# The exponential's shift in an attention kernel, made by one VectorE pass over the scores in place of a maximum and an addition

## The chip, the cores and the metric

One core of one Trainium2 chip runs the whole program. The metric is the device time of one execution in microseconds, as the median of the runs of a kernel. The engines are named as in the profile: PE is TensorE's matmuls, PEld its weight loads, DVE is VectorE, ACT is ScalarE, POOL is GpSimd, SP is the queue that issues most of the DMAs.

## What is computed

For each of 32 batches, 112 latents (`x`, normalized) attend to 375 context rows and to themselves (487 keys), with 16 heads of 64 dimensions; then comes a routed feed-forward layer of 8 experts. The part that matters here is the softmax:

```
q = lat @ Wq;  k, v = split(concatenate([ctx, lat]) @ Wkv)
dots = einsum('bhid,bhjd->bhij', q, k) * scale          # 112 x 487 per head
attn = softmax(dots, axis=-1)
out  = einsum('bhij,bhjd->bhid', attn, v) @ Wout
x    = x + tanh(g_xattn) * out
```

The exponential is taken of a score less its row's maximum, plus a constant, `P_SHIFT` = 14 ln 2, which drops out when a row is divided by its sum.

## The kernel before

The program is `attention()`, which ends at about 1363 us, and then `routed_ffn()`, which the change does not touch. Attention works in steps `t`; a step is one pair of heads (two heads, h = 0 and 1) of a batch, so a batch has 8 steps, j = 0 to 7. All engines walk the same list of steps (L639 for PE, L502 for DVE, L376 for ACT, L288 for POOL, L208 for SP), each with its own program written out by hand in a fixed order; semaphores tie them together. Nothing is reordered at run time.

Precision is made of pieces: q and k are split into a high part, which ACT copies out of PSUM, and a low part, which DVE computes as PSUM less the high part (`k_lo` L530, `q_lo` L518). V is split likewise (`v_sb` L416 on ACT, L536 on DVE), and so is P (`p_parts`: L374 on ACT, L279 on POOL).

In an even step t PE makes the scores of two pairs, t and t+1, into four PSUM banks (L653), after `exp_done` says that the banks are free. Then, in every step, PE projects K and V for the same pair of the next batch (L635, twelve matmuls in all), and multiplies P of pair t - 4 by V (L684, L686). In steps with j = 2 and 4 it transposes the normalized inputs of the batch after the next (L719, L720, called T), and in steps with j = 3 and 7 it projects half of Q. K, V, T and Q units share two PSUM banks, `proj_ps`, in turn: the function `take` (L617) makes a unit wait until the unit before the last has been read out by its last reader. So the K projection of an odd step waits for `k_lo` of the even step before it; T waits for `k_lo` of its own step, and the K projection after T waits for the low part of V.

DVE's order in an even step is: `q_lo` if due (j = 0 and 4), four maxima (L495, one per bank) with two additions of `P_SHIFT` among them (L500, each over two columns of `neg_max`), then `k_lo`, then the low part of V, then the rest. L500 waits for the semaphore `max_done` of DVE's own maxima. ACT's order in an even step is: high part of K, exponential h = 0, high part of V, attention output's high part (L424), exponential h = 1. In the odd step: exponential h = 0, K, exponential h = 1, V, and then the four copies of P (L374), of which two fall in the next even step. An exponential writes `p_f` in SBUF and its row sum through the accumulator, which the trace shows as a second instruction (ACTIVATION_READ_ACCUMULATOR, L365). ACT waits for `bias_done` ahead of h = 0 alone.

SP transposes P of two pairs in each even step by DMA (L217), once POOL has made their low parts.

Of the kernel before, what the change touches and what calls it, by code (L numbers as in the profile page):

```python
# [6 lines left out]
F16 = mybir.dt.float16  # L7
I32 = mybir.dt.int32
U32 = mybir.dt.uint32
ALU = mybir.AluOpType  # L10
ACT = mybir.ActivationFunctionType
AX = mybir.AxisListType

NB, LQ, LC, D = 32, 112, 375, 256
H, DH = 16, 64
LK = LC + LQ
# [11 lines left out]
P_SHIFT = 14 * 0.6931471805599453  # L28
# [5 lines left out]
def span(t):  # L34

    return t // NP, t % NP
# [6 lines left out]
def is_pair(p):  # L43
    return 0 <= p < PAIRS


def is_batch(b):
    return 0 <= b < NB
# [20 lines left out]
def attention(nc, x, ctx_in, g_x, ln_m_g, ln_m_b, ln_l_g, ln_l_b, wq, wkv, wout, gate_w, x2_out, xn_out, top_v, top_i, ident, w1, w2, peaks):  # L69
    with ExitStack() as st:  # L70
        sb = lambda name, shape, dt=F32: st.enter_context(nc.sbuf_tensor(name, shape, dt))
        sem = lambda name: st.enter_context(nc.semaphore(name))
# [18 lines left out]
        scale = scale_i[:, 0].bitcast(F32)  # L91
        inverse = scale_i[:, 1].bitcast(F32)
        undo = sb("att_undo", [128, 6])
# [17 lines left out]
        p_f = sb("p_f", [128, 2, 2, 512])  # L111
        p_parts = sb("p_parts", [128, PS, 2, 2, 512], F16)
        pt_sb = sb("pt_sb", [128, PS, 16 * LQ + 16], F16)
        neg_max = sb("neg_max", [128, 2, 4])
        shift = sb("shift", [128, 2, 4])
        row_sum = sb("row_sum", [128, 4, 4])
        inv_sum = sb("inv_sum", [128, 4, 4])
# [16 lines left out]
        scores_ps = [bank(f"scores_ps{n}") for n in range(4)]  # L134
# [12 lines left out]
        proj_done = sem("proj_done")  # L147
        kq_high = sem("kq_high"); kq_low = sem("kq_low"); v_high = sem("v_high"); v_low = sem("v_low")
        kv_affine = sem("kv_affine"); kvhi_done = sem("kvhi_done"); kvlo_done = sem("kvlo_done")
        scores_done = sem("scores_done"); max_done = sem("max_done"); bias_done = sem("bias_done"); exp_done = sem("exp_done")  # L150
        p_high = sem("p_high"); p_low = sem("p_low"); p_moved = [sem(f"p_moved{n}") for n in range(PS)]
        pv_done = sem("pv_done"); inv_done = sem("inv_done"); o_summed = sem("o_summed"); o_scaled = sem("o_scaled"); o_high = sem("o_high"); o_low = sem("o_low")
        o_moved = [sem("o_moved0"), sem("o_moved1")]
# [11 lines left out]
        def unit_ready(kind, index):  # L165

            n = UNIT_NUMBER[kind, index]
            return n + 1, proj_ps[n % 2]
# [181 lines left out]
        @block.scalar  # L350
        def _(act):
            act.wait_ge(small_loaded, 16 * 6)
            act.activation(tanh_g[:, :], tanh_g[:, :], ACT.Tanh).then_inc(tanh_done, 1)
            act.wait_ge(scales_ready, 1)
            for k in range(KD):
                act.activation(wkv_hi[:, k], stage[:, k], ACT.Copy, scale=scale[:, 0:1]).then_inc(w_high, 1)

            def exponential(p, h):
                if h == 0:
                    act.wait_ge(bias_done, p + 1)  # L360
                    if p >= 2:

                        act.wait_ge(p_low, 2 * (p - 2) + 2)
                n = 2 * (p % 2) + h
                act.activation(p_f[0:LQ, p % 2, h, 0:LK], scores_ps[n][0:LQ, 0:LK], ACT.Exp, bias=shift[0:LQ, p // 2 % 2, n:n + 1],  # L365
                               accum_out=row_sum[0:LQ, p // 2 % 4, n:n + 1]).then_inc(exp_done, 1)

            def p_high_of(p):
                if p >= PS:

                    act.wait_ge(p_moved[p % PS], 16 * (p // PS))
                for h in range(2):
                    act.wait_ge(exp_done, 2 * p + h + 1)
                    act.activation(p_parts[0:LQ, p % PS, h, 0, 0:LK], p_f[0:LQ, p % 2, h, 0:LK], ACT.Copy).then_inc(p_high, 1)  # L374

            for t in STEPS:  # L376
                b, j = span(t)
                qb = b if j == 0 else b + 1
                if t == -NP - 2:
                    act.activation(wq_hi[:, :, :], stage_q, ACT.Copy, scale=scale[:, 1:2]).then_inc(w_high, 1)  # L380
                    act.activation(wout_hi[:, :, :], stage_out, ACT.Copy, scale=scale[:, 2:3]).then_inc(w_high, 1)
                if t == 0:
                    act.wait_ge(set_up, 2)
                if j in (0, 4) and is_batch(qb):

                    n = 1 if j == 0 else 0
                    done, ps = unit_ready("Q", 2 * qb + n)
                    act.wait_ge(proj_done, done)
                    act.activation(q_hi[:, 4 * n:4 * n + 4], ps[:, 0:4 * LQ].rearrange("p (m q) -> p m q", m=4), ACT.Copy,
                                   scale=undo[:, 0:1]).then_inc(kq_high, 1)  # L390
                if t % 2 == 0 and is_pair(t - 1):
                    p_high_of(t - 1)
                ob = out_batch(t, 3 * NP + 2)
                if ob is not None:
                    act.wait_ge(xnt_done, ob + 1)
                    act.activation(xnt_sb[:, :, :], tail_ps[:, 0:KD * LQ].rearrange("p (k q) -> p k q", k=KD), ACT.Copy).then_inc(xnt_copied, 1)
                if t % 2 == 1 and is_pair(t):
                    exponential(t, 0)
                if is_pair(t + NP):
                    done, ps = unit_ready("K", t + NP)  # L400
                    act.wait_ge(proj_done, done)
                    act.activation(k_hi[:, j], ps[:, 0:LKP], ACT.Copy).then_inc(kq_high, 1)  # L402
                if j in (3, 5) and is_batch(b + 2):
                    k = (j - 3) // 2
                    act.wait_ge(kv_affine, 2 * (b + 2) + k + 1)
                    act.activation(kv_hi[:, b % 2, k], kv_f[:, k], ACT.Copy).then_inc(kvhi_done, 1)
                if is_pair(t):
                    exponential(t, t % 2)
                if is_pair(t + NP):
                    done, ps = unit_ready("V", t + NP)  # L410
                    act.wait_ge(proj_done, done)
                    c, half_ = j % KT, j // KT
                    rows = 128 if c < KT - 1 else LKP - 128 * (KT - 1)
                    if b in (-1, 0) and j == 0:
                        act.wait_ge(v_cleared, b + 2)
                    act.activation(v_sb[0:rows, (b + 1) % 2, c, 8 * half_:8 * half_ + 8, 0], ps[0:rows, :].rearrange("p (n d) -> p n d", d=DH),  # L416
                                   ACT.Copy, scale=V_SCALE).then_inc(v_high, 1)
                g = (t - LAG - 2) // 2
                if t % 2 == 0 and 0 <= g < PAIRS // 2:
                    ob, n = g // 4, g % 4  # L420
                    act.wait_ge(o_scaled, g + 1)
                    if n == 0 and ob >= 2:
                        act.wait_ge(o_moved[ob % 2], 16 * (ob // 2))
                    act.activation(o_parts[0:LQ, ob % 2, 0, 4 * DH * n:4 * DH * (n + 1)], o_f[0:LQ, g % 2].rearrange("p h d -> p (h d)"), ACT.Copy).then_inc(o_high, 1)  # L424
                if t % 2 == 0 and is_pair(t):
                    exponential(t, 1)
                if t % 2 == 1 and is_pair(t - 1):
                    p_high_of(t - 1)

        @block.vector  # L430
        def _(dve):
# [4 lines left out]
            def then(instruction):  # L436
                n_step[0] += 1
                instruction.then_inc(scale_step, 1)

                dve.wait_ge(scale_step, n_step[0])  # L440

            def weight_scales():
# [27 lines left out]
                then(dve.tensor_scalar(affine[:, :, :].rearrange("p a k -> p (a k)"), affine[:, :, :].rearrange("p a k -> p (a k)"), scale[:, 3:4], None, ALU.mult))  # L470
                then(dve.tensor_tensor(undo[:, 2:3], inverse[:, 3:4], inverse[:, 0:1], ALU.mult))
                then(dve.tensor_scalar(undo[:, 3:4], undo[:, 2:3], inverse[:, 2:3], 1.0 / V_SCALE, ALU.mult, ALU.mult))
                then(dve.tensor_scalar(undo[:, 4:5], undo[:, 2:3], inverse[:, 3:4], float(DH) ** -0.5, ALU.mult, ALU.mult))
                then(dve.tensor_scalar(undo[:, 0:1], undo[:, 4:5], inverse[:, 1:2], None, ALU.mult))
                dve.wait_ge(tanh_done, 1)
                then(dve.tensor_scalar(undo[:, 1:2], undo[:, 3:4], tanh_g[:, :], None, ALU.mult))
# [12 lines left out]
                dve.wait_ge(w_high, 4)  # L489
                dve.scalar_tensor_tensor(out=wout_lo[:, :, :], in0=stage_out, scalar=scale[:, 2:3], in1=wout_hi[:, :, :], op0=ALU.mult, op1=ALU.subtract).then_inc(w_ready, 1)  # L490

            def maximum(p, h):
                n = 2 * (p % 2) + h
                dve.wait_ge(scores_done, 2 * p + h + 1)
                dve.tensor_reduce(neg_max[0:LQ, p // 2 % 2, n:n + 1], scores_ps[n][0:LQ, 0:LK], AX.X, ALU.max, negate=True).then_inc(max_done, 1)  # L495

            def bias(p):
                n = 2 * (p % 2)
                dve.wait_ge(max_done, 2 * p + 2)
                dve.tensor_scalar(shift[0:LQ, p // 2 % 2, n:n + 2], neg_max[0:LQ, p // 2 % 2, n:n + 2], P_SHIFT, None, ALU.add).then_inc(bias_done, 1)  # L500

            for t in STEPS:  # L502
                b, j = span(t)
                nb = b + 2
                if t == -3 * NP + 2:
                    weight_scales()
# [7 lines left out]
                if j in (0, 4) and is_batch(qb):  # L514
                    n = 1 if j == 0 else 0
# [2 lines left out]
                    dve.scalar_tensor_tensor(out=q_lo[:, 4 * n:4 * n + 4], in0=ps[:, 0:4 * LQ].rearrange("p (m q) -> p m q", m=4), scalar=undo[:, 0:1],  # L518
                                             in1=q_hi[:, 4 * n:4 * n + 4].bitcast(F32), op0=ALU.mult, op1=ALU.subtract).then_inc(kq_low, 1)
                if t % 2 == 0 and is_pair(t):  # L520
                    maximum(t, 0)
                    maximum(t, 1)
                    maximum(t + 1, 0)
                    bias(t)
                    maximum(t + 1, 1)
                    bias(t + 1)
                if is_pair(t + NP):
                    done, ps = unit_ready("K", t + NP)
                    dve.wait_ge(kq_high, kq_count("K", t + NP))
# [789 lines left out]
```

## Time and profile before

| | us |
|---|---|
| median of 3 runs | 1902.32 |
| lowest and highest | 1900.02, 1903.77 |
| the profiled execution, its own time | 1902.62 |
| its span | 1900.9 |
| PE busy in the span | 1674.2 (88%) |
| DVE busy | 1428.0 (75%) |
| ACT busy | 1195.3 (63%) |
| POOL busy | 1183.0 (62%) |

The span in 40 equal slices shows attention up to slice 28 or so and the feed-forward layer behind it:

```profile
PE   2899999999999999999999999998402999999980
DVE  4777888888888888888888888877395666666646
ACT  2587777777777777877777777777254333433320
POOL 4477777777777777777777777767263343333320
PEclk9999999999999999999999999999555999999995
```

Each digit is the busy share of a slice in tenths, and the last line is the clock granted to TensorE. Times of a trace are counted from the span's start. A matmul's recorded length is modelled and longer than the distance to the next one, so a gap on PE is best read from starts, or from the idle time ahead of a weight load.

### The profile page before, as it was taken

The page shows a single profiled execution, that of the slowest core. Times are in us where ns is not written, and L with a number is a line of the kernel's source. Part 1 is how long each engine was busy: PE and PEld are TensorE (multiplying, and loading weights), DVE is VectorE, ACT ScalarE, POOL GpSimd, SP SyncE. Part 2 cuts the span into 40 slices and gives each one's busy share as a digit, 9 for nine tenths or more (in the row PEclk, how much of TensorE's full clock was granted, in tenths as well). Part 3 has the DMA queues.
Part 4 walks back from the last instruction along what each step waited for, and adds up shares of the span by engine and source line. Part 5 has one row for each costly group of instructions (what it writes and reads, how often), then busy time and mean ns, then how long its engine had stood idle before and what let it go on. Part 6 is the DMA issues. An engine that isn't in the chain of part 4 may idle for free. (4 is left out here: it accounts for less than half of the span.)

```text
span 1900.9 us, 42714 instructions
## 1 busy us (share of the span) xinstructions
PE 1674.2 (88%) x15031; PEld 1163.1 (61%) x15032; DVE 1428.0 (75%) x2917; ACT 1195.3 (63%) x2666; POOL 1183.0 (62%) x1297
## 2 busy tenths in 40 slices
PE   2899999999999999999999999998402999999980
PEld 1456666666666666666666666665302999989970
DVE  4777888888888888888888888877395666666646
ACT  2587777777777777877777777777254333433320
POOL 4477777777777777777777777767263343333320
PEclk9999999999999999999999999999555999999995
DMA  3267766767767666676776776767455111111119
GB/s 131 46 127 140 142 144 131 139 139 142 147 129 145 138 140 144 135 139 138 139 150 136 136 137 129 138 130 142 118 186 173 46 49 45 50 50 47 47 35 289
DMA packets 599541, 233.18 MB, mean 123 GB/s; under 512 B 534064, under 2 KB 584016, under 8 KB 598992
## 3 DMA queue, kind: packets, MB, share of 16 engines
q1 hardware_dynamic: 592656, 212.67, 52.5%
q0 software_dynamic: 6720, 18.36, 3.1%
q8 instruction: 98, 1.61, 0.3%
q14 instruction: 67, 0.55, 0.1%
HBM read 78.66 MB, written 20.19 MB: 52 GB/s over the span
## 5 line engine op out<-in xcount | busy, mean ns | idle before, releaser
L279 POOL TENSOR_TENSOR p_parts<-p_f,p_parts 112x487 f16<-112x487 f32 x512 | 560.4, 1118 | 194.2 <-ACT p_parts L374 194.2
L365 ACT ACTIVATE p_f<-scores_ps,shift 112x487 f32<-112x487 f32 x512 | 337.0, 663 | 13.3 <-DVE shift L500 9.7
L495 DVE TENSOR_REDUCE neg_max<-scores_ps 112x1 f32<-112x487 f32 x512 | 313.0, 654 | 27.1 <-PE scores_ps L653 27.1
L402 ACT ACTIVATE k_hi<-proj_ps 128x488 fp32r<-128x488 f32 x256 | 147.9, 578 | 262.5 <-PE proj_ps L635 262.5
L1018 ACT ACTIVATE space<-h_ps,b_sb,undo 128x256 f32<-128x256 f32 x280 | 142.8, 560 | 232.1 <-PE h_ps L1247 228.8
L374 ACT ACTIVATE p_parts<-p_f 112x487 f16<-112x487 f32 x512 | 275.9, 607 | 0.0
L536 DVE SCALAR_TENSOR_TENSOR v_sb<-proj_ps,v_sb 128x512 f16<-128x512 f32 (+1 forms) x256 | 176.5, 689 | 92.1 <-ACT v_sb L416 89.4
L530 DVE TENSOR_TENSOR k_lo<-proj_ps,k_hi 128x488 fp32r<-128x488 f32 x256 | 168.2, 657 | 78.2 <-ACT k_hi L402 78.0
L684 PE MATMUL pv_ps<-v_sb,pt_sb 128*128 128x128 f16 x2048 | 218.9, 221 | 7.8 <-DMA pt_sb<-p_parts 7.8
L635 PE MATMUL proj_ps<-kv_hi,wkv_hi 128*128 128x488 f16 x512 | 192.3, 376 | 22.0 <-POOL kv_lo L306 13.5
L635 PE MATMUL proj_ps<-wkv_hi,kv_hi 128*128 128x512 f16 (+1 forms) x512 | 194.6, 380 | 0.1
L635 PE MATMUL proj_ps<-wkv_lo,kv_hi 128*128 128x512 f16 (+1 forms) x512 | 194.6, 380 | 0.0
L635 PE MATMUL proj_ps<-wkv_hi,kv_lo 128*128 128x512 f16 (+1 forms) x512 | 194.6, 380 | 0.0
L635 PE MATMUL proj_ps<-kv_lo,wkv_hi 128*128 128x488 f16 x512 | 189.7, 370 | 0.0
L635 PE MATMUL proj_ps<-kv_hi,wkv_lo 128*128 128x488 f16 x512 | 189.5, 370 | 0.0
L1270 PE MATMUL y_ps<-w_hi,stage 128*128 x1120 | 189.0, 273 | 0.0
L989 POOL DMA_INDIRECT y_rows<-space,y_row_i x70 | 69.6, 994 | 152.0 <-DVE space L1187 141.3
L416 ACT ACTIVATE v_sb<-proj_ps 128x512 f16<-128x512 f32 (+1 forms) x256 | 152.5, 596 | 16.9 <-PE proj_ps L635 6.4
L1247 PE MATMUL h_ps<-xt_hi,w_hi 128*128 128x256 f16 x560 | 154.4, 276 | 4.3 <-DVE xt_lo L1179 4.3
L684 PEld LDWEIGHTS pv_ps<-v_sb,pt_sb 128*128 128x128 f16 x2048 | 135.1, 99 | 37.6 <-DMA pt_sb<-p_parts 8.9
L1247 PE MATMUL h_ps<-xt_lo,w_hi 128*128 128x256 f16 x560 | 154.5, 276 | 0.0
L1247 PE MATMUL h_ps<-xt_hi,w_lo 128*128 128x256 f16 x560 | 154.3, 276 | 0.0
(222 smaller groups left out, 4075.1 us busy)
## 6 DMA issues: line engine op xcount, KB each, us to landing
w_part<-in_L_ffn_w_dram SPq DMA_DIRECT2D x64, 256.0 KB, 3.5
stage<-in_L_ffn_w_dram SPq DMA_DIRECT2D x32, 512.0 KB, 4.1
ctx_sb<-in_ctx_dram SPq DMA_DIRECT2D x32, 375.0 KB
space<-y_rows SPq DMA_DIRECT2D x32, 224.0 KB, 4.7
pt_sb<-p_parts SPq DMA_TRANSPOSE x256, 4.0
x_sb<-in_x_dram SPq DMA_DIRECT2D x32, 112.0 KB
res_sb<-in_x_dram SPq DMA_DIRECT2D x32, 112.0 KB, 5.3
x_dram<-x_sb SPq DMA_DIRECT2D x32, 112.0 KB, 2.9
```

Source lines behind the costliest of these rows:

```text
L279: pool.tensor_tensor(p_parts[0:LQ, p % PS, h, 1, 0:LK], p_f[0:LQ, p % 2, h, 0:LK], p_parts[0:LQ, p % PS, h, 0, 0:LK], ALU.subtract).then_i ...
L365: act.activation(p_f[0:LQ, p % 2, h, 0:LK], scores_ps[n][0:LQ, 0:LK], ACT.Exp, bias=shift[0:LQ, p // 2 % 2, n:n + 1], accum_out=row_sum[0: ...
L374: act.activation(p_parts[0:LQ, p % PS, h, 0, 0:LK], p_f[0:LQ, p % 2, h, 0:LK], ACT.Copy).then_inc(p_high, 1)
L402: act.activation(k_hi[:, j], ps[:, 0:LKP], ACT.Copy).then_inc(kq_high, 1)
L416: act.activation(v_sb[0:rows, (b + 1) % 2, c, 8 * half_:8 * half_ + 8, 0], ps[0:rows, :].rearrange("p (n d) -> p n d", d=DH), ACT.Copy, sc ...
L495: dve.tensor_reduce(neg_max[0:LQ, p // 2 % 2, n:n + 1], scores_ps[n][0:LQ, 0:LK], AX.X, ALU.max, negate=True).then_inc(max_done, 1)
L530: dve.tensor_tensor(k_lo[:, j], ps[:, 0:LKP], k_hi[:, j].bitcast(F32), ALU.subtract).then_inc(kq_low, 1)
L536: dve.scalar_tensor_tensor(out=v_of(1), in0=ps[0:rows, :].rearrange("p (n d) -> p n d", d=DH), scalar=V_SCALE, in1=v_of(0), op0=ALU.mult, ...
L635: last = nc.tensor.matmul(out, lhs(a, k), rhs(c, k), start=(n == 0), stop=(n == 3 * KD - 1))
L684: last = nc.tensor.matmul(pv_ps[:, at:at + 128], block_of(0, c), v_sb[:, sv, c, n].rearrange("p a d -> p (a d)"), start=(c == 0), stop=(c ...
L1247: last = nc.tensor.matmul(h_ps[m][:, c * ROWS:c * ROWS + ROWS], (w1_hi, w1_lo)[a][:, k, bass.ds(e1, 1), f:f + 128].rearrange("p o f -> p ( ...
L1270: last = nc.tensor.matmul(y_ps[s][:, r * D:r * D + D], (g_hi, g_lo)[a][:, s, m, c, r * 128:r * 128 + 128], (w2_hi, w2_lo)[b][:, m * 2 + c, ...
```

## The change

The maximum of a row and the addition of `P_SHIFT` become one instruction, a tensor_scalar with an accumulator output: it adds `P_SHIFT` to each score, writes the 112 x 487 result as float16 into a new SBUF tile, `passed`, that nothing reads, and accumulates the minimum of what it passes. So that a minimum serves, the scores are negated: the factor `undo[:, 4]`, from which q's scale is made, gets a minus sign, and the exponential reads its input with scale -1. ACT now waits for `shift_done` ahead of each exponential.

```
-  then(dve.tensor_scalar(undo[:, 4:5], undo[:, 2:3], inverse[:, 3:4], float(DH) ** -0.5, ALU.mult, ALU.mult))
+  then(dve.tensor_scalar(undo[:, 4:5], undo[:, 2:3], inverse[:, 3:4], -float(DH) ** -0.5, ALU.mult, ALU.mult))
...
   def exponential(p, h):
-      if h == 0:
-          act.wait_ge(bias_done, p + 1)
-          if p >= 2:
-              act.wait_ge(p_low, 2 * (p - 2) + 2)
+      act.wait_ge(shift_done, 2 * p + h + 1)
+      if h == 0 and p >= 2:
+          act.wait_ge(p_low, 2 * (p - 2) + 2)
       act.activation(p_f[...], scores_ps[n][0:LQ, 0:LK], ACT.Exp, bias=shift[...],
+                     scale=-1.0,
                      accum_out=row_sum[...]).then_inc(exp_done, 1)
...
-  def maximum(p, h):
+  def shifted_minimum(p, h):
       n = 2 * (p % 2) + h
       dve.wait_ge(scores_done, 2 * p + h + 1)
-      dve.tensor_reduce(neg_max[...], scores_ps[n][0:LQ, 0:LK], AX.X, ALU.max, negate=True).then_inc(max_done, 1)
-  def bias(p):
-      n = 2 * (p % 2)
-      dve.wait_ge(max_done, 2 * p + 2)
-      dve.tensor_scalar(shift[..., n:n + 2], neg_max[..., n:n + 2], P_SHIFT, None, ALU.add).then_inc(bias_done, 1)
+      dve.tensor_scalar(passed[0:LQ, n], scores_ps[n][0:LQ, 0:LK], P_SHIFT, None, ALU.add, ALU.min,
+                        accum_out=shift[..., n:n + 1]).then_inc(shift_done, 1)
...
   if t % 2 == 0 and is_pair(t):
-      maximum(t, 0)
-      maximum(t, 1)
-      maximum(t + 1, 0)
-      bias(t)
-      maximum(t + 1, 1)
-      bias(t + 1)
+      for p in (t, t + 1):
+          for h in range(2):
+              shifted_minimum(p, h)
```

## Rows read from the trace of the kernel before

**Rows 1.** The page's first line.

```profile
span 1900.9 us, 42714 instructions
```

**Rows 2.** Busy time by stretch: us, each engine's busy us, granted clock, DMA share.

```profile
700.00:1000.00 300.00, 296.85 (x2698) 188.32 (x2696) 251.08 (x559) 234.61 (x552) 230.76 (x264) 1.00 0.70 141
```

**Rows 3.** Groups of DVE instructions, 100 to 1300 us: busy us, mean ns, idle before.

```profile
L495 DVE TENSOR_REDUCE neg_max<-scores_ps 112x1 f32<-112x487 f32 x484 | 295.8, 654 | 21.1 <-PE scores_ps L653 21.1
L500 DVE TENSOR_SCALAR shift<-neg_max 112x2 f32<-112x2 f32 x242 | 95.1, 393 | 4.2
```

**Rows 4.** Waits of PE's weight loads, 100 to 1300 us: total, times, longest.

```profile
PEld proj_ps L635 <- DVE k_lo L530: 15.7, 61, 1.7
PEld proj_ps L719 <- DVE k_lo L530: 15.7, 29, 0.6
```

**Rows 5.** Timeline of DVE and PEld in a step with j = 0: start, us.

```profile
709.14 1.80 DVE L495 TENSOR_REDUCE neg_max<-scores_ps 112x1 f32<-112x487 f32 x3
710.86 0.17 DVE L500 TENSOR_SCALAR shift<-neg_max 112x2 f32<-112x2 f32 x1
710.94 0.65 DVE L495 TENSOR_REDUCE neg_max<-scores_ps 112x1 f32<-112x487 f32 x1
711.62 0.47 DVE L500 TENSOR_SCALAR shift<-neg_max 112x2 f32<-112x2 f32 x1
712.01 0.65 DVE L530 TENSOR_TENSOR k_lo<-proj_ps,k_hi 128x488 fp32r<-128x488 f32 x1
...
712.71 0.10 PEld L635 LDWEIGHTS proj_ps<-kv_hi,wkv_hi 128*128 128x128 f16 x1 [0.22 <-DVE k_lo L530]
```

**Rows 6.** Timeline of POOL in the same step.

```profile
709.89 2.19 POOL L279 TENSOR_TENSOR p_parts<-p_f,p_parts 112x487 f16<-112x487 f32 x2
```

**Rows 7.** Timeline of DVE, ACT and PEld in the step with j = 4.

```profile
727.76 1.80 DVE L495 TENSOR_REDUCE neg_max<-scores_ps 112x1 f32<-112x487 f32 x3
...
730.95 0.65 DVE L530 TENSOR_TENSOR k_lo<-proj_ps,k_hi 128x488 fp32r<-128x488 f32 x1
731.53 0.67 DVE L536 SCALAR_TENSOR_TENSOR v_sb<-proj_ps,v_sb 128x512 f16<-128x512 f32 x1
...
730.57 0.19 ACT L365 ACTIVATION_READ_ACCUMULATOR p_f<-scores_ps,shift 112x1 f32 x1
730.66 0.59 ACT L416 ACTIVATE v_sb<-proj_ps 128x512 f16<-128x512 f32 x1
...
731.66 0.31 PEld L719 LDWEIGHTS proj_ps<-ident,norm_sb 125*128 125x128 f32 x3 [0.55 <-DVE k_lo L530]
...
732.25 0.10 PEld L635 LDWEIGHTS proj_ps<-kv_hi,wkv_hi 128*128 128x128 f16 x1 [0.18 <-DVE v_sb L536]
```

**Rows 8.** Timeline of DVE, ACT and PEld in the step with j = 6.

```profile
739.14 1.81 DVE L495 TENSOR_REDUCE neg_max<-scores_ps 112x1 f32<-112x487 f32 x3 [0.72 <-PE scores_ps L653]
...
742.39 0.65 DVE L530 TENSOR_TENSOR k_lo<-proj_ps,k_hi 128x488 fp32r<-128x488 f32 x1
...
741.15 0.58 ACT L402 ACTIVATE k_hi<-proj_ps 128x488 fp32r<-128x488 f32 x1 [3.24 <-PE proj_ps L635]
...
743.10 0.10 PEld L635 LDWEIGHTS proj_ps<-kv_hi,wkv_hi 128*128 128x128 f16 x1 [0.19 <-DVE k_lo L530]
```

**Rows 9.** Timeline of DVE and PE in the step with j = 2.

```profile
717.64 1.77 DVE L495 TENSOR_REDUCE neg_max<-scores_ps 112x1 f32<-112x487 f32 x3
...
720.40 0.65 DVE L530 TENSOR_TENSOR k_lo<-proj_ps,k_hi 128x488 fp32r<-128x488 f32 x1
...
721.34 0.52 PE L719 MATMUL proj_ps<-ident,norm_sb 125*128 125x125 f32 x3
```

**Rows 10.** Groups of DVE instructions in the feed-forward layer, 1450 to 1900 us.

```profile
L1177 DVE TENSOR_SCALAR xt_hi<-xt_ps 128x512 f16<-128x512 f32 x35 | 23.9, 682 | 7.3 <-PE xt_ps L1256 7.3
```

**Rows 11.** The last batch: an ACT wait (1296 to 1363 us) and a stretch.

```profile
ACT p_f L365 <- DVE shift L500: 6.1, 4, 2.2
...
1310.00:1320.00 10.00, 8.36 (x77) 6.71 (x78) 6.00 (x12) 7.36 (x20) 7.40 (x8) 0.69 0.94 202
```

More of the change, by code:

```diff
@@ L113, in attention @@
         pt_sb = sb("pt_sb", [128, PS, 16 * LQ + 16], F16)
-        neg_max = sb("neg_max", [128, 2, 4])
+        passed = sb("passed", [128, 4, LK], F16)
         shift = sb("shift", [128, 2, 4])
@@ L149, in attention @@
         kv_affine = sem("kv_affine"); kvhi_done = sem("kvhi_done"); kvlo_done = sem("kvlo_done")
-        scores_done = sem("scores_done"); max_done = sem("max_done"); bias_done = sem("bias_done"); exp_done = sem("exp_done")
+        scores_done = sem("scores_done"); shift_done = sem("shift_done"); exp_done = sem("exp_done")
         p_high = sem("p_high"); p_low = sem("p_low"); p_moved = [sem(f"p_moved{n}") for n in range(PS)]
@@ L358, in exponential @@
             def exponential(p, h):
-                if h == 0:
-                    act.wait_ge(bias_done, p + 1)
-                    if p >= 2:
-                        act.wait_ge(p_low, 2 * (p - 2) + 2)
+                act.wait_ge(shift_done, 2 * p + h + 1)
+                if h == 0 and p >= 2:
+                    act.wait_ge(p_low, 2 * (p - 2) + 2)
                 n = 2 * (p % 2) + h
-                act.activation(p_f[0:LQ, p % 2, h, 0:LK], scores_ps[n][0:LQ, 0:LK], ACT.Exp, bias=shift[0:LQ, p // 2 % 2, n:n + 1],
+                act.activation(p_f[0:LQ, p % 2, h, 0:LK], scores_ps[n][0:LQ, 0:LK], ACT.Exp, bias=shift[0:LQ, p // 2 % 2, n:n + 1], scale=-1.0,
                                accum_out=row_sum[0:LQ, p // 2 % 4, n:n + 1]).then_inc(exp_done, 1)
@@ L490, in split_out_weights @@
                 dve.scalar_tensor_tensor(out=wout_lo[:, :, :], in0=stage_out, scalar=scale[:, 2:3], in1=wout_hi[:, :, :], op0=ALU.mult, op1=ALU.subtract).then_inc(w_ready, 1)
-            def maximum(p, h):
+            def shifted_minimum(p, h):
                 n = 2 * (p % 2) + h
                 dve.wait_ge(scores_done, 2 * p + h + 1)
-                dve.tensor_reduce(neg_max[0:LQ, p // 2 % 2, n:n + 1], scores_ps[n][0:LQ, 0:LK], AX.X, ALU.max, negate=True).then_inc(max_done, 1)
-            def bias(p):
-                n = 2 * (p % 2)
-                dve.wait_ge(max_done, 2 * p + 2)
-                dve.tensor_scalar(shift[0:LQ, p // 2 % 2, n:n + 2], neg_max[0:LQ, p // 2 % 2, n:n + 2], P_SHIFT, None, ALU.add).then_inc(bias_done, 1)
+                dve.tensor_scalar(passed[0:LQ, n], scores_ps[n][0:LQ, 0:LK], P_SHIFT, None, ALU.add, ALU.min,
+                                  accum_out=shift[0:LQ, p // 2 % 2, n:n + 1]).then_inc(shift_done, 1)
             for t in STEPS:
```

## The prediction

> **What bounds the kernel now.** The page gives a span of 1900.9 us [rows 1]; the execution's own time is 1902.6, within 0.02% of the median of the runs (1902.3), so the sum below is made against 1902.6. The view by stretches shows that attention is TensorE's: in 300 us it is busy for 296.9, at the full granted clock, while DVE is busy for 251 and ACT for 235 [rows 2]. A faster DVE can therefore only give back what PE loses by waiting for DVE. The view of the waits shows two such groups of PE's weight loads, both on `k_lo`: 15.7 us ahead of projections and 15.7 us ahead of transposes [rows 4]. That is the pool from which the change can draw, some 31 us in 1200, and the timelines show why `k_lo` is late: it stands behind the four maxima and the two additions.
>
> **What the block costs now.** From the first maximum to `k_lo` it is 712.01 - 709.14 = 2.87 us at j = 0 [rows 5], 720.40 - 717.64 = 2.76 at j = 2 [rows 9], 3.19 at j = 4 [rows 7] and 3.25 at j = 6 [rows 8]. Three maxima take from 709.14 to 710.86, that is 0.573 from start to start, though one is recorded with 0.654 [rows 3, 5]. Four would be 2.29, so the additions and their waits cost 0.47 to 0.96 a block. That is a lot for two columns each. The mean addition lasts 393 ns [rows 3], and the short one took 0.17, with the next maximum 0.08 after its start; the long one lasted from 711.62 to 712.09 [rows 5], and POOL's two subtractions lasted from 709.89 to 712.08 [rows 6]. The short one ended at 711.03, in the middle of POOL's two, where one gives way to the other. The addition goes from SBUF to SBUF, and it looks as if it stood until POOL's instruction was over.
>
> The Trainium skill, SBUF — State Buffer, has in the section on the shared ports that a tensor_scalar in a two-port mode and a GpSimd instruction block each other fully, whichever came first, and that the form with an accumulator output is not among the ops that do. By that rule the long additions are waits for a port, and the new form, which has one, waits for none; the trace agrees on the first half, and nothing in it shows the second.
>
> **What the change adds.** The pass itself: the nearest row is a tensor_scalar from PSUM to float16, 682 ns for 512 columns [rows 10], against 654 for a maximum over 487 [rows 3]; the 25 columns more account for the 28 ns at about 1 ns each, so I take the same 0.573 from start to start. Beside it comes the reading of the accumulator, which no DVE row shows. Below, it could cost nothing. Above, it could wait for the recorded end of the pass (0.654 - 0.573 = 0.08 later) and then take its own 0.2, as ACT's does by its recorded length: 0.28. On ACT the next instruction starts 0.09 after that reading (730.57 to 730.66) [rows 7], and DVE's short addition let the next one start after 0.08 [rows 5]; I take 0.08, since both rows are of that kind of short instruction. A block is then 4 x (0.573 + 0.08) = 2.61 us.
>
> The Trainium skill, VectorE: DVE Perf Modes, speaks against such fusing: its section on the DRAIN says that the next op starts only when the pipe is empty, and that one should lower the number of ops; its section on two Vector instructions with no wait between them counts an accumulator output as an instruction of its own. A block would go from six instructions to eight. The maxima here start 0.08 ahead of the recorded end of the one before, so the trace does not show a full drain; if the reading had one, the block would be near the upper bound, which is the slower rival below.
>
> **What each step of a batch gives.** At j = 0, `k_lo` starts 0.26 earlier (2.87 - 2.61). The K projection of the next step idles 0.22 for it [rows 5], so all of the 0.22 goes. At j = 6, `k_lo` could start 0.64 earlier, at 741.75; the high part of K is done at 741.73 [rows 8], so that does not hold it up. The 0.19 of idle time goes whole. At j = 4, `k_lo` starts 0.58 earlier, at 730.37, and the 0.55 ahead of the transposes goes [rows 7]. But a part comes back: the K projection after them waits for the low part of V, which now ends at 732.20 and releases PE at 732.25. It follows ACT's high part, over at 731.25, so it can run from about 731.28 to 731.96 and release PE at 732.01: 0.24 is left of the 0.55. That is the new wait, on ACT in place of DVE. If ACT's copy came earlier too, since its exponential no longer waits for an addition, the most would be 0.54, where the 0.59 of transposes [rows 7] starts straight after the products with V. At j = 2, `k_lo` ends at 721.05 and the transposes start at 721.34 anyway [rows 9]: nothing, and 0.2 us of slack. The odd steps have no block. Sum: 0.22 + 0.19 + 0.24 = 0.65 us a batch. K is projected beside the scores in 31 of the 32 batches: 20.2 us.
>
> **What costs nothing.** The negation is a sign in a constant and a scale in an instruction that ACT runs anyway. The wait ahead of the second exponential is met long before, as ACT comes to it over 1 us after the pass. DVE's float16 writes into `passed` have no reader, and no DMA is touched. What covers the first exponential in the body is the K copy ahead of it. In the last batch there is no projection, and ACT does wait for the addition: 6.1 us in four waits [rows 11]. With the change the first exponential needs one pass of 0.65 instead of three and an addition. But the DMA engines that transpose P are 0.94 busy there [rows 11], so most of it will turn into waiting for them. I credit 2 us, between 0 and 6.1.
>
> **The sum:** 1902.6 - 20.2 - 2.0 = 1880.4; against the median 0.3 less, and I say 1880.5.
>
> **Rivals.** (A) *The reading of the accumulator is dear* and DVE becomes later than it was. At 0.28 each a block is 4 x 0.853 = 3.41 us, and `k_lo` comes 0.54, 0.65, 0.22 and 0.16 later at j = 0, 2, 4 and 6. The slack of 0.2 at j = 2 takes its part off: 0.54 + 0.45 + 0.22 + 0.16 = 1.37 a batch, 42 us, so 1945. The point from which it decides: at 0.19 a block is 3.05, which loses 0.18 and 0.09 at j = 0 and 2 and gains some 0.14 and 0.19 at j = 4 and 6, about nothing. For it speaks that no DVE row shows the instruction; against it that the twin on ACT lets the next one start after 0.09. Chance 0.12.
> (B) *A middling price*, about 0.15: the block is 2.89 and j = 0 gives nothing (2.87 before), while j = 4 and 6 give 0.24 and 0.19: 0.43 x 31 = 13.3, and 1 at the end, so 1888. The same time comes out if the price is small and PE meets another wait at one of the steps. Chance 0.20.
> (C) *Nothing reaches PE*, because another reader of the two banks is late wherever `k_lo` was: 1902 within 4 us. Against it: the three waits named are put down to `k_lo` in 90 cases [rows 4]. Chance 0.08. That the additions stay in another form is excluded by the diff, which takes the instructions out.
>
> **Numbers.** The forecast has 0.60. The low end: 0.22 + 0.19 + 0.54 for 31 batches and 6.1 at the end would be 1867; all of these together is unlikely, and I set 1872. The high end takes in (B) with a price up to 0.18: 1898. What is left out is (A) and most of (C). A measurement of this kernel can tell 0.2% (3.8 us) from no change; faster by more: 0.60 + 0.20 = 0.80, the same 0.08, slower 0.12.
>
> **What would show it.** In the profile after: a second DVE instruction behind each pass, with the next pass 0.65 after the one before; `k_lo` 2.6 us after the block's start at all j alike, since POOL no longer sets its length; the waits for `k_lo` ahead of L719 and L635 gone or below 3 us each, and the one for the low part of V still there, but put down to ACT's copy; DVE busy less by roughly the additions' 100 us, less the readings. Wrong: a pass spacing above 0.75 (then A), or the spacing as said with PE's waits unchanged (then C).

## The result and the profile after

The kernel after takes 1880.9 us in the median of 4 runs (1878.3 to 1881.2), the kernel before beside it 1902.0. The ratio is 0.9886, with a 95% interval of 0.9870 to 0.9902: faster by 21 us.

Page and busy time by stretch of the kernel after, for [rows 1, 2]:

```profile
span 1879.1 us, 42970 instructions
...
700.00:1000.00 300.00, 297.52 (x2741) 191.98 (x2739) 233.73 (x617) 235.56 (x559) 235.53 (x269) 1.00 0.69 141
```

In the same 300 us there are 43 matmuls more (2741 against 2698): PE does the same work with fewer holes. DVE is busy for 234 us in place of 251. Its groups, 100 to 1280 us, stand against [rows 3]:

```profile
L494 DVE TENSOR_SCALAR_CACHE_REDUCE passed<-scores_ps 112x487 f16<-112x487 f32 x484 | 291.1, 658 | 21.1 <-PE scores_ps L645 21.1
...
L494 DVE DVE_READ_ACCUMULATOR passed<-scores_ps 112x1 f32 x484 | 39.6, 82 | 0.0
```

The pass lasts as long as the maximum did (658 and 654 ns). The timeline of DVE, ACT and PEld in the step with j = 4, for [rows 7]:

```profile
713.66 0.65 DVE L494 TENSOR_SCALAR_CACHE_REDUCE passed<-scores_ps 112x487 f16<-112x487 f32 x1
714.24 0.08 DVE L494 DVE_READ_ACCUMULATOR passed<-scores_ps 112x1 f32 x1
714.24 0.66 DVE L494 TENSOR_SCALAR_CACHE_REDUCE passed<-scores_ps 112x487 f16<-112x487 f32 x1
714.82 0.08 DVE L494 DVE_READ_ACCUMULATOR passed<-scores_ps 112x1 f32 x1
...
715.41 0.66 DVE L494 TENSOR_SCALAR_CACHE_REDUCE passed<-scores_ps 112x487 f16<-112x487 f32 x1
715.99 0.08 DVE L494 DVE_READ_ACCUMULATOR passed<-scores_ps 112x1 f32 x1
715.99 0.66 DVE L522 TENSOR_TENSOR k_lo<-proj_ps,k_hi 128x488 fp32r<-128x488 f32 x1
717.17 0.69 DVE L528 SCALAR_TENSOR_TENSOR v_sb<-proj_ps,v_sb 128x512 f16<-128x512 f32 x1 [0.52 <-ACT v_sb L415]
...
716.54 0.60 ACT L415 ACTIVATE v_sb<-proj_ps 128x512 f16<-128x512 f32 x1
...
716.96 0.31 PEld L711 LDWEIGHTS proj_ps<-ident,norm_sb 125*128 125x128 f32 x3
...
717.91 0.10 PEld L627 LDWEIGHTS proj_ps<-kv_hi,wkv_hi 128*128 128x128 f16 x1 [0.53 <-DVE v_sb L528]
```

Four passes now take 715.99 - 713.66 = 2.33 us, where the block took 3.19. The transposes (L711) follow PE's work with no wait, and the projection behind them waits for the low part of V, which itself stands 0.52 behind ACT's copy. The reading of the accumulator starts in the same instant as the next pass and is recorded with 0.08, but the passes start 0.585 apart in place of the maxima's 0.573: pass and reading together cost 0.01 us more than a maximum, not 0.08.

At j = 0, 2 and 4 `k_lo` starts 2.31 to 2.34 after the block's start. At j = 6 it is 2.62, since `k_lo` now waits there for the high part of K:

```profile
724.80 0.67 DVE L494 TENSOR_SCALAR_CACHE_REDUCE passed<-scores_ps 112x487 f16<-112x487 f32 x1 [0.72 <-PE scores_ps L645]
...
727.42 0.67 DVE L522 TENSOR_TENSOR k_lo<-proj_ps,k_hi 128x488 fp32r<-128x488 f32 x1 [0.19 <-ACT k_hi L401]
```

The waits of the weight loads, 100 to 1280 us, for [rows 4]:

```profile
PEld proj_ps L627 <- DVE v_sb L528: 16.5, 31, 0.5
...
PEld proj_ps L627 <- DVE k_lo L522: 2.2, 2, 1.1
```

Both waits for `k_lo` are gone, but for two cases at the start. The wait for the low part of V was 5.3 us before and is 16.5 now. To see the period of a batch, take the first output matmul of two batches in a row; before, and then after:

```profile
735.48 0.27 PE L699 MATMUL tail_ps<-wout_hi,ot_sb 128*128 128x256 f16 x1
...
775.32 0.27 PE L699 MATMUL tail_ps<-wout_hi,ot_sb 128*128 128x256 f16 x1
```

```profile
721.13 0.27 PE L691 MATMUL tail_ps<-wout_hi,ot_sb 128*128 128x256 f16 x1
...
760.32 0.27 PE L691 MATMUL tail_ps<-wout_hi,ot_sb 128*128 128x256 f16 x1
```

39.84 us became 39.19. Over the 27 regular batches of each trace the mean period is 39.85 and 39.18, and no batch is more than 0.03 off: 0.66 a batch. Attention ends, and the feed-forward layer's first activation runs, here (before, after):

```profile
1365.86 0.20 ACT L994 ACTIVATE tanh_f<-tanh_f 128x1 f32<-128x1 f32 x1 [4.72 <-DMA tanh_f<-in_g_ffn_dram]
```

```profile
1342.23 0.20 ACT L986 ACTIVATE tanh_f<-tanh_f 128x1 f32<-128x1 f32 x1 [4.71 <-DMA tanh_f<-in_g_ffn_dram]
```

So attention gave 23.6 us, and 1.9 came back in the untouched feed-forward layer (535.0 us from there to the span's end before, 536.9 after). That is within the spread of that part: in the twelve kernels below, which do not touch it either, it is between 534.1 and 537.9.

### The profile page after: what moved, and what is told of

It is laid out like the page before. It is cut to its first block and busy times, and to the rows that moved or that the text cites. A ratio compares the mean times of both kernels' runs of the same rounds, so it can differ in the third digit from the quotient of the medians.

```text
span 1879.1 us, 42970 instructions
## 1 busy us (share of the span) xinstructions
PE 1657.4 (88%) x15031; PEld 1161.6 (62%) x15032; DVE 1348.8 (72%) x3173; ACT 1186.2 (63%) x2666; POOL 1185.2 (63%) x1297
## 5 line engine op out<-in xcount | busy, mean ns | idle before, releaser
L494 DVE TENSOR_SCALAR_CACHE_REDUCE passed<-scores_ps 112x487 f16<-112x487 f32 x512 | 308.0, 658 | 30.2 <-PE scores_ps L645 30.2
```

Of the source, the lines that this page charges most:

```text
L494: dve.tensor_scalar(passed[0:LQ, n], scores_ps[n][0:LQ, 0:LK], P_SHIFT, None, ALU.add, ALU.min, accum_out=shift[0:LQ, p // 2 % 2, n:n + 1] ...
```

## The experiments

The theory: the gain is the length of the block ahead of `k_lo`, and nearly all of what was shortened were the two-column additions, standing until POOL was done with an instruction, for a port that both use. Rivals: the exponentials come earlier (one wait each, as soon as one pass is done); DVE simply has less work; the fused pass is better by itself. Ratios are against the kernel before, timed beside each. The period is the mean of the regular batches.

| kernel | median us | ratio, 95% interval | period, us |
|---|---|---|---|
| before | 1902.0 | | 39.85 |
| after | 1880.9 | 0.9870 to 0.9902 | 39.18 |
| one-column additions | 1880.2 | 0.9873 to 0.9906 | 39.20 |
| after, coarse waits | 1880.7 | 0.9875 to 0.9908 | 39.18 |
| after, sham additions | 1927.0 | 1.0115 to 1.0148 | 40.7 |
| after, one-column shams | 1880.0 | 0.9872 to 0.9908 | 39.20 |
| second addition late | 1933.9 | 1.0143 to 1.0178 | 40.9 or 41.9 |
| the same, one column | 1883.4 | 0.9891 to 0.9924 | 39.27 |
| no addition | 1878.3 | 0.9858 to 0.9891 | 39.18 |
| after, five passes | 1891.7 | 0.9929 to 0.9962 | 39.49 |
| after, six passes | 1963.0 (1 run) | | 41.66 |
| before, output early | 1878.5 | 0.9867 to 0.9900 | 39.00 |
| after, output early | 1867.0 | 0.9793 to 0.9826 | 38.70 |
| one column, output early | 1867.4 | 0.9801 to 0.9834 | 38.72 |

**Additions over one column.** The kernel before, with maxima and all:

```
-  dve.tensor_scalar(shift[..., n:n + 2], neg_max[..., n:n + 2], P_SHIFT, None, ALU.add).then_inc(bias_done, 1)
+  dve.tensor_scalar(shift[..., n:n + 1], neg_max[..., n:n + 1], P_SHIFT, None, ALU.add)
+  dve.tensor_scalar(shift[..., n + 1:n + 2], neg_max[..., n + 1:n + 2], P_SHIFT, None, ALU.add).then_inc(bias_done, 1)
```

> The kernel before, each addition over two columns made as two additions over one column. Theory (a two-column addition takes a port that POOL uses and waits for POOL's instruction): a one-column addition doesn't, lasts about 0.16 us and lets the next start after 0.07 to 0.08; the block falls to 4 x 0.573 + 4 x 0.075 + 0.115 = 2.7 us at every j, and the time to 1882 to 1888, though DVE has 256 instructions more. Rival (additions are long for what they wait on, or as any small operation behind a reduction): each is as long as before, the block grows by 0.16 or more, and the time is 1902 to 1915.

1880.2 us, 2 under the range expected. The block of a step with j = 2, DVE and then POOL:

```profile
705.28 1.77 DVE L495 TENSOR_REDUCE neg_max<-scores_ps 112x1 f32<-112x487 f32 x3
706.97 0.14 DVE L500 TENSOR_SCALAR shift<-neg_max 112x1 f32<-112x1 f32 x1
707.03 0.14 DVE L501 TENSOR_SCALAR shift<-neg_max 112x1 f32<-112x1 f32 x1
707.09 0.65 DVE L495 TENSOR_REDUCE neg_max<-scores_ps 112x1 f32<-112x487 f32 x1
707.78 0.15 DVE L500 TENSOR_SCALAR shift<-neg_max 112x1 f32<-112x1 f32 x1
707.85 0.14 DVE L501 TENSOR_SCALAR shift<-neg_max 112x1 f32<-112x1 f32 x1
707.91 0.66 DVE L531 TENSOR_TENSOR k_lo<-proj_ps,k_hi 128x488 fp32r<-128x488 f32 x1
...
706.99 2.18 POOL L279 TENSOR_TENSOR p_parts<-p_f,p_parts 112x487 f16<-112x487 f32 x2
```

Four additions of one column take 0.06 to 0.07 each between starts, and with the wait for the last maximum the block is 2.63; two of two columns together cost 0.47 to 0.96 [rows 5, 7 to 9]. The additions of one column run through POOL's instruction (the last two lie inside its 706.99 to 709.17) without waiting for it. With more instructions than before and the same waits between engines, the whole of the gain is there. The fused pass is one way of getting it, not its cause. The kernel before shows the wait in every case: of its 256 additions 191 last over 0.2 us, and each of these ends 21 to 28 ns behind the recorded end of an instruction of POOL; the three that started while POOL was idle last 0.16 to 0.17.

The Trainium skill, SBUF — State Buffer, section Who interferes with whom, puts such blocking on the two-port form of tensor_scalar and exempts the accumulator form. The traces agree on both halves: the endings just given, and in the kernel after 512 passes that all last between 0.63 and 0.67 us. What they show is the wait and its end; that a port is waited for is the skill's account of it.

**Coarse waits in the kernel after.** ACT waits ahead of h = 0 alone, for three passes (pair t) or four (pair t+1), as it did before:

```
-  act.wait_ge(shift_done, 2 * p + h + 1)
+  if h == 0:
+      act.wait_ge(shift_done, 2 * p + (3 if p % 2 == 0 else 2))
```

> The kernel after, with ACT's waits as coarse as before: the first exponential of a block only after three passes, that of pair t+1 only after all four. Theory: in the body nothing changes (period 39.18 us), since the copy of K covers it; in the last batch 1 to 3 us come back: 1881 to 1884. Rival 1 (earlier exponentials): most of the 21 us comes back, 1895 to 1902.

1880.7 us and the same period: earlier exponentials are worth nothing in the body, and the 1 to 3 us that were expected back in the last batch did not come either.

**Sham additions in the kernel after,** over two columns and then over one, at the places of the old ones (the semaphore orders writes to the same tile, one block apart):

```
+  if p == t + 1:
+      dve.wait_ge(sham_done, t)
+      dve.tensor_scalar(spare[0:LQ, h], half[0:LQ, 0:2], P_SHIFT, None, ALU.add).then_inc(sham_done, 1)
```

> The kernel after, with two additions over two columns of SBUF put at the places of the old ones; nothing reads what they write, and they wait for nothing of their own block. Theory: they wait for POOL's port (mean about 0.4 us, up to 1) and make the block 2.34 + 0.2 + 0.35 = 2.9 us, near the 2.98 of before; the period returns to about 39.7 and the time to 1895 to 1900. Rival 1 (earlier exponentials) or a gain by the form of the pass itself: 1881 to 1884. If a small instruction costs only its 0.07, the block is 2.5 and the time stays at 1881.

1927.0 us: the direction was right, the size was not. The shams last 555 ns in the mean, longer than the 393 of the real ones, because they meet POOL at another point. At j = 2, DVE and POOL:

```profile
732.01 1.11 DVE L522 TENSOR_SCALAR spare<-half 112x2 f32<-112x2 f32 x1
...
731.98 2.19 POOL L280 TENSOR_TENSOR p_parts<-p_f,p_parts 112x487 f16<-112x487 f32 x2
```

POOL started 0.03 earlier, and two columns stood for the whole first instruction of its pair. Before the change it was the addition that came a moment first at that place (719.34, POOL's pair 719.35; its block was the shortest, 2.76 us [rows 9]). At j = 0, 4 and 6 the blocks have the lengths of before, 2.85, 3.18 and 3.25, though they are made of passes, since POOL's instructions end them; only the one at j = 2 is longer, 3.82, and with it the period.

> The kernel after with the sham additions of the earlier run, each made as two of one column. Theory (it is the port, not a small instruction in that place): four instructions of 0.07 us each make the block 2.62 us, under what the steps can take, so the period stays at 39.18 to 39.22 and the time at 1879 to 1883, against 1927 with the two-column shams. Rival (any instruction put there costs, or the semaphore does): above 1895.

1880.0 us, with shams of 0.14 to 0.15. Four more instructions of one column at those places cost nothing; two of two columns cost 46 us.

**The second addition late.** The kernel before, with `bias(t + 1)` moved behind the low part of V:

```
   maximum(t + 1, 1)
-  bias(t + 1)
   ...
   dve.scalar_tensor_tensor(out=v_of(1), ...).then_inc(v_low, 1)
+  if t % 2 == 0 and is_pair(t):
+      bias(t + 1)
```

> The kernel before, with all its maxima and additions; only the second addition of a block (pair t+1) moves behind the low part of V. Theory (the change gains by the length of the block ahead of k_lo): k_lo then starts about 2.4 to 2.7 us after the block's start in place of 2.8 to 3.25, which is enough for the waits at j = 0, 4 and 6, so the batch's period falls from 39.85 us to about 39.2 and the time to 1881 to 1885, as after the change. Rival 1 (the gain comes from earlier exponentials): these come no earlier here, so 1902. Rival 2 (the gain comes from 100 us less of DVE work): DVE's work is the same, so 1902.

1933.9 us, a plain miss: `k_lo` came early as foreseen (2.33 to 2.75 after the block's start), but the moved addition did more harm elsewhere. In a step with j = 0, DVE, POOL and ACT:

```profile
733.43 1.86 DVE L500 TENSOR_SCALAR shift<-neg_max 112x2 f32<-112x2 f32 x1
...
733.17 0.67 POOL L285 TENSOR_TENSOR o_parts<-o_f,o_parts 112x256 f16<-112x256 f32 x1 [0.98 <-ACT o_parts L424]
733.79 1.47 POOL L311 TENSOR_TENSOR norm_sb<-norm_sb,rstd 125x768 f32<-125x768 f32 x1
...
735.32 0.67 ACT L365 ACTIVATE p_f<-scores_ps,shift 112x487 f32<-112x487 f32 x1 [1.58 <-DVE shift L500]
```

It stood from 733.43 to 735.29, through the end of one POOL instruction and the whole of the next, and the exponential of the odd step waited 1.58 for it. DVE's later work came late too, and there PE loses the most, in a wait that the kernel before does not have (weight loads, 100 to 1280 us):

```profile
PEld tail_ps L706 <- DVE xn_sb L574: 28.6, 27, 1.1
```

So the rule for this kernel is not only where an addition stands but what POOL does then. With one column in the same late place:

> The late second addition of the earlier run (1934), with all additions of one column. Theory: its 32 us of loss came from two-column additions that stood behind two POOL instructions in a row (up to 1.87 us), with ACT and DVE waiting; with one column the order does no harm: 1878 to 1884. Rival (the later place itself delays the exponentials of the odd step): the time stays above 1905.

1883.4 us. The 50 us between the two are the second column's; the late place itself costs some 3 (1883.4 against 1880.2).

**No addition.** The maximum goes straight into `shift`, and the constant `P_SHIFT` is left out. ACT waits for one maximum ahead of each exponential, as the kernel after does for one pass; the coarse waits above show that this is worth nothing.

> The kernel before without any addition: the negated maximum is the shift, and the constant 14 ln 2 is left out (it drops out at the division, but for what float16 keeps of small values). The block is 4 x 0.573 = 2.29 us, 0.04 less than after the change. Theory: the waits it could take away at j = 0, 4 and 6 are gone already at 2.33, so it is within 1.5 us of the kernel after: 1880 to 1882. Rival (the form of the pass matters, or DVE's total work): it differs from the kernel after by more than 3 us.

1878.3 us, 2.6 from the kernel after where at most 1.5 were expected, but with the same period: the body is equal, and of the 2.4 us between the two spans 1.8 lie in the feed-forward layer (535.1 and 536.9). A block of 2.28 is worth no more than one of 2.34 or 2.66.

**More passes,** one or two ahead of the last pass, with results that nothing reads:

```
+  if p == t + 1 and h == 1:
+      dve.wait_ge(sham_done, t // 2 * 1)
+      dve.wait_ge(scores_done, 2 * t + 4)
+      dve.tensor_scalar(junk[0:LQ, 0], scores_ps[3][0:LQ, 0:LK], P_SHIFT, None, ALU.add, ALU.min,
+                        accum_out=spare[0:LQ, 0:1]).then_inc(sham_done, 1)
```

> The kernel after with a fifth pass in each block, ahead of the last, whose result nothing reads. The block is 2.92 us. Theory: k_lo is then late by 0.26 at j = 0, by 0.09 at j = 2 and 0.19 at j = 4 beyond what the steps can take, nothing at j = 6: 0.54 x 31 = 17 us on the 1881, so 1893 to 1902. Rival (cost in proportion to DVE's work, 128 x 0.585 = 75 us, or none, since DVE is busy for 72% only): 1955 or 1881.

> As the five passes, with six: the block is 3.50 us, and past every slack each further 0.585 us of a block is paid whole: late by 0.84, 0.67, 0.77 and 0.43 at the four even steps, 2.7 a batch, 84 us: 1950 to 1968. It gives the slope of the slower rival of the prediction (a dear accumulator reading), whose block of 3.41 was put at 1945. Rival (DVE has room): 1900 or less.

1891.7 us, 1.3 under the range expected, and 1963.0. The fifth pass costs 0.30 us a batch where 0.54 was expected. The weight loads' waits with five passes, 100 to 1270 us:

```profile
PEld proj_ps L635 <- DVE k_lo L530: 12.0, 32, 1.7
PEld proj_ps L719 <- DVE k_lo L530: 8.5, 29, 0.3
...
PEld proj_ps L635 <- DVE v_sb L536: 5.8, 29, 0.2
```

The first of them is 0.29 a batch at j = 0, the loss itself. The second stands at j = 4, but it takes the place of the wait for the low part of V, which was 16.5 and is 5.8, so the 0.19 expected there was not lost, nor the 0.09 at j = 2. The sixth pass costs 2.17, nearly its full 4 x 0.585 = 2.34. The first is nearly free and the second is paid whole: that is how a block behind slack behaves, and neither DVE's total work nor its busy share would say it.

**The output product early.** PE does 6 of its 24 matmuls at j = 4, ahead of the transposes:

```
-  ob = out_batch(t, NP + 13)
-  if ob is not None:
+  for ob, steps in ((out_batch(t, NP + 12), range(0, 2)), (out_batch(t, NP + 13), range(2, NP))):
+      if ob is None:
+          continue
...
-      for i in range(NP):
+      for i in steps:
...
-      last.then_inc(out_done, 1)
+      if i == NP - 1:
+          last.then_inc(out_done, 1)
```

> The kernel after, with the first quarter of the output product (6 of 24 matmuls, about 0.64 us) done at j = 4 ahead of the transposes in place of j = 5. After the change the K projection behind these transposes waits some 0.4 us a batch for the low part of V, which follows ACT's copy. Theory: work in front covers the wait, the matmul total stays, the period falls from 39.18 to about 38.8 and the time to 1868 to 1873. Rival (the wait only moves, to the block at j = 6 or to the exponentials ahead of the scores): 1879 to 1883.

1867.0 us, better than both kernels and 1 under the range expected. The waits of the weight loads, 100 to 1270 us:

```profile
PEld proj_ps L627 <- DVE kv_f L539: 14.1, 55, 0.3
...
PEld proj_ps L627 <- DVE k_lo L522: 2.2, 2, 1.1
PEld proj_ps L627 <- DVE v_sb L528: 1.6, 3, 0.5
```

The 16.5 us ahead of the projection are down to 1.6. The weight loads wait longer for `kv_f` (5.7 us after the change), but PE's matmuls do not: that wait is not among PE's own. The same edit in the two other kernels:

> The kernel before, additions and all, with a quarter of the output product ahead of the transposes at j = 4. Theory: the 0.53 and 0.11 us that PE loses there are covered by 0.64 us of work, the losses at j = 0 and 6 (0.21, 0.18) stay: 0.6 x 31 = 19 us less, 1880 to 1886; the rest of what the best version has comes from the additions. Rival (the additions fall against POOL in another way, as in the two kernels that came out slow): a time off that by more than 5 us, to either side, with additions of another mean length than 0.39.

> The kernel before with additions of one column and a quarter of the output product early; the maxima stay. Theory: the fused pass has nothing of its own beyond the port it doesn't take, so this equals the kernel after with the output early (1867.0): 1865 to 1870. Rival (the shorter block of the fused pass, 2.33 against 2.7 us, is worth something once the wait at j = 4 is covered): 1872 or more.

1878.5 us for the kernel before with its additions (1.5 us under the range expected; its additions last 348 ns in the mean, not 393, as they fall against POOL in another way: the block at j = 6 is 2.84 in place of 3.25, and its wait of 0.19 is gone), and 1867.4 for the one with one-column additions and no fused pass. The edit at j = 4 and the one of the additions are each worth some 22 us alone and 35 together, because both take the wait at j = 4; with the long additions the early output takes the one at j = 6 as well.

## Why the prediction was right

**The time.** 1880.5 was forecast, 1880.9 measured. Some of the closeness is luck: the 2 us of the last batch were not had and nearly as much came from the ramp at the start, and the spread of the parts outside cancelled too.

**The bound.** It stood as read: PE is the limit, and what it lost by `k_lo` was the pool. Of the 31.4 us of waits [rows 4] 2.2 are left, and 16.5, where it was 5.3, stand ahead of the projection at j = 4, as the step on the part that comes back had it (PE released at 732.01 for 732.25, so most of the wait turns into one for ACT's copy).

**The body.** 0.65 us a batch forecast, 0.66 measured; 20.5 us in 31 batches.

**The price of the reading.** I took 0.08 from ACT's and from DVE's short addition; it is 0.01, so a block is 2.34 and not 2.61. It changed nothing, since past 2.65 (2.87 less the 0.22 at j = 0) the steps had no more to give; the kernel with one-column additions, at 2.63 to 2.67, has the same period within 0.02. That `k_lo` starts 2.62 after the block's start at j = 6 fits the forecast's number and not its reason: there it is the high part of K that holds it up, which at 2.61 was said not to. The nearest rows were too dear, and so rival (A) and the middling (B) lost their ground. Eight instructions (2.34 us) cost less than six (2.76 to 3.25), and a pass starts 0.07 ahead of the recorded end of the one before, so no full drain stands between them. The Trainium skill, VectorE: DVE Perf Modes, section The DRAIN you can't avoid, says what the prediction left out, that a next op which is not held starts earlier; the 0.07 agrees.

**The cause of the long additions.** It was argued from one ending (712.09 beside 712.08) and has been shown since by the endings of all 191 long ones, and by one against two columns in four pairs of kernels.

**The last batch.** The 2 us credited there were not had. The waits ahead of ACT's exponentials were 6.1 us for additions [rows 11] and 1.4 for POOL's subtraction; after, they are (1280 to 1345 us):

```profile
ACT p_f L364 <- DVE passed L494: 4.2, 3, 3.3
ACT p_f L364 <- POOL p_parts L279: 3.5, 4, 1.0
```

That is 7.7 in place of 7.5: what the first exponentials gained came back as waits for POOL, and one pass, whose scores came late, was waited for 3.3. The prediction had the part that comes back as a wait for the DMA engines.

Attention's end lies 23.6 us earlier (1365.86 to 1342.23), and 20.5 are the body's; the first scores already came 1.5 earlier, before any maximum has run, which the change cannot have done (in the kernel after with the output early, whose setup is the same, they come at 73.4):

```profile
L653 PE MATMUL scores_ps<-k_hi,q_hi x512: 376/468/746, 73.2 to 1325.4; 64*112 64x488 f32 x171
```

```profile
L645 PE MATMUL scores_ps<-k_hi,q_hi x512: 376/468/742, 71.7 to 1304.3; 64*112 64x488 f32 x171
```

What remains, some 1.6 us, is the ramp at the start, where batches are not yet regular and the weight loads wait more for `k_lo` (60 to 180 us: 11.2 us before, 6.4 after). The first output matmul starts 5.1 earlier (177.7 and 172.5); 1.5 of that are the setup's, and some 1.8, by my estimate from the body's 0.66 a batch, the regular share of the steps up to it. I had no term for the ramp. It stood in for the last batch, and the feed-forward layer's 1.9 took the setup's 1.5 back.

## What to carry to other kernels

When an operation over a few columns lasts many times its sisters, compare its end with the ends of the other engine's instructions before blaming the instruction; here one column at a time removed a wait that two columns had, with no other change. What shortening such a block is worth is read from the consumer: add up what PE idles for it, and see which producer is due next, since the rest of the gain lies in covering that one. And an engine's order that looks harmless can be wrong by tens of microseconds while it holds operations whose length depends on the phase of a neighbour: make them independent first, then move them.

## What was not expected of the hardware

The reading of the accumulator on DVE is recorded with 82 ns, and a pass with it starts only 12 ns later than the next maximum would, while ACT's lets the next instruction start only after 90.

A two-column addition that waits gets in, as a rule, when POOL's current instruction ends, even where POOL's next follows at once. In the kernel before 98 additions started within the first of POOL's two subtractions; the longest took 0.99 us, and all were over 21 to 28 ns behind that first one's end. But it can be passed over. Of the 1024 two-column operations in the traces of the four kernels that have them (before, before with the output early, the shams, the late addition), 29 stood through a whole further instruction of POOL behind the one that they met: all with the late addition, and all where `norm_sb` follows `o_parts` (the one above started at 733.43, POOL's next at 733.79, and it ended at 735.29). What decides it was not tried.

Where both start at nearly the same time, hundredths of a microsecond decide. In the kernel before and in the one with the output early, each addition that started 0.010 to 0.026 us ahead of POOL's subtraction behind `o_f` lasted 0.16; the shams that started 0.017 to 0.031 behind it lasted 1.1. With the late addition, where it started 0.001 to 0.014 ahead, both happened. That is why the block at j = 2 was the shortest in the kernel before and the longest with the shams.
